# Three of eight row groups summed by TensorE and copied out by ScalarE, the last two groups normalised in one step, and six groups routed first: one gated cross-attention and expert block

## The reference, cut to what matters

```python
# x: (4, 1024, 256); ctx: (4, 77, 256); mask: (1, 1024, 77); 8 experts
x = x + tanh(g_xattn[0]) * xattn(layernorm(x), ctx, ctx, mask, W1, b1, W2, b2)
x = x + tanh(g_ffn[0])   * ffn(layernorm(x), router_w, router_b, w1, w2)

def xattn(q, k, v, mask, ...):          # both projections on q and on k, none on v
    qk = proj(q) @ proj(k).T * 256 ** -0.5 + mask
    return softmax(qk) @ v

def ffn(h, ...):                        # one expert for a token
    route = softmax(h @ router_w + router_b)
    e = argmax(route)
    a, g = split(h @ w1[e])             # 256 -> 2 * 1024
    return (silu(a) * g @ w2[e]) * max(route)
```

## Time and profile before

| what | us |
|---|---|
| median of 3 runs | 448.74 |
| the runs | 448.74, 452.37, 445.57 |
| the profiled execution, as timed | 449.49 |
| its span, first to last instruction | 447.70 |
| PE busy | 401.3 (90% of the span) |
| DVE / ACT / POOL busy | 217.0 / 176.5 / 243.7 |

### The profile page before, as it was taken

The page is one execution under the profiler, slowest core; times in us unless marked ns, Lnnn a source line. Parts: engine busy times, 40 slices in busy tenths (PEclk is TensorE's granted clock), DMA queues, the critical chain, the costliest instruction groups (busy, mean ns, idle before and its releaser), DMA issues.

```text
span 447.7 us, 9834 instructions
## 1 busy us (share of the span) xinstructions
PE 401.3 (90%) x2431; PEld 346.5 (77%) x2432; DVE 217.0 (48%) x527; ACT 176.5 (39%) x338; POOL 243.7 (54%) x324
## 2 busy tenths in 40 slices
PE   5998984149989999999999999999999999999990
PEld 4787872027878888888888888888888888888880
DVE  4689899933454443444433444433444434444340
ACT  1167650024443454545532344445433543233230
POOL 2356997221865577887772258728852676232221
PEclk9999897559999999999999999999999999999996
DMA  7950233863333044333442003433331011000010
GB/s 204 360 199 2 95 107 131 85 175 108 118 118 117 23 166 163 135 117 116 134 155 83 27 17 117 134 112 124 117 117 35 4 35 35 24 24 27 24 33 12
DMA packets 29850, 44.01 MB, mean 98 GB/s; under 512 B 8377, under 2 KB 25581, under 8 KB 27791
## 3 DMA queue, kind: packets, MB, share of 16 engines
q1 hardware_dynamic: 24095, 34.45, 24.6%
q0 software_dynamic: 3456, 9.11, 6.3%
q10 hardware_dynamic: 2288, 0.33, 0.5%
HBM read 35.44 MB, written 8.83 MB: 99 GB/s over the span
## 4 chain that ended last, share of the span: by engine, by line
PE 80%; DVE 7%; POOL 6%; DMA 2%; issue 2%; ACT 1%; DVEq 0%; SPq 0%; POOLq 0%; ACTq 0%
PE py L1117 22%; PE pa L1099 21%; PE pg L1099 21%; PE ph L1109 7%; POOL w_lo L415 2%; PE px L1084 2%; DVE x_all L742 1%; PE ps_s L1024 1%; POOL rstd L399 1%; DMA ctx_in<-in_ctx 1%; DVE bn L750 1%; DMA x_sorted<-residual_rows,idx_gather 1%; PE ps_p L968 1%; PE ps_xt L940 1%; DVE x_norm L878 1%
## 5 line engine op out<-in xcount | busy, mean ns | idle before, releaser
L895 DVE TENSOR_TENSOR ht_lo<-ph,ht_hi 128x512 fp32r<-128x512 f32 x70 | 48.4, 691 | 135.4 <-ACT ht_hi L624 135.4
L493 POOL TENSOR_TENSOR w_lo<-staging,w_hi x84 | 107.1, 1304 | 7.3 <-ACT w_hi L645 4.0
L624 ACT CAST ht_hi<-ph 128x512 fp32r<-128x512 f32 x70 | 41.1, 586 | 118.6 <-PE ph L1109 83.4
L1117 PE MATMUL py<-w_hi,ht_hi 128*128 x280 | 81.3, 291 | 0.8 <-DVE out_tile L903 0.8
L1117 PE MATMUL py<-w_lo,ht_hi 128*128 x280 | 78.4, 280 | 0.0
L1117 PE MATMUL py<-w_hi,ht_lo 128*128 x280 | 78.3, 280 | 0.0
L482 POOL DMA_INDIRECT out<-out_tile,idx_now x34 | 34.6, 1019 | 72.6 <-DVE out_tile L903 72.0
L1099 PE MATMUL pa<-w_hi,xt_hi 128*128 (+1 forms) x140 | 58.7, 420 | 0.8 <-ACT xt_hi L606 0.8
L443 POOL DMA_INDIRECT x_sorted<-residual_rows,idx_now x34 | 35.6, 1048 | 39.5 <-DVE x_norm L878 21.4
L1099 PE MATMUL pg<-w_lo,xt_hi 128*128 (+1 forms) x140 | 55.9, 400 | 0.0
L1099 PE MATMUL pg<-w_hi,xt_hi 128*128 (+1 forms) x140 | 55.9, 399 | 0.0
(11 more groups left out here) (168 smaller groups left out, 583.2 us busy)
## 6 DMA issues: line engine op xcount, KB each, us to landing
staging<-in_L_ffn_w SPq DMA_DIRECT2D x24, 1024.0 KB
residual_rows<-x_all SPq DMA_DIRECT2D x8, 516.0 KB, 4.0
x_all<-in_x SPq DMA_DIRECT2D x8, 512.0 KB, 10.1
x_sorted<-residual_rows,idx_now POOLq DMA_INDIRECT x34
out<-out_tile,idx_now POOLq DMA_INDIRECT x34, 2.5
w_in<-in_L_xattn_W SPq DMA_DIRECT2D x2, 256.0 KB, 4.7
ctx_in<-in_ctx SPq DMA_DIRECT2D x1, 308.0 KB
mask_in<-in_fside_1xSxS ACTq DMA_DIRECT2D x1, 308.0 KB, 11.7
```

What stands on the lines that cost most here:

```text
L493: lo = nc.gpsimd.tensor_tensor(out=w_lo[:, bass.ds(dst + q * QW, QW)], in0=staging[:, bass.ds(src + q * QW, QW)], in1=w_hi[:, bass.ds(dst ...
L624: nc.scalar.copy(ht_hi[:, j], ph[j][:]).then_inc(hhi_ready[j], 1)
L895: nc.vector.tensor_tensor(out=ht_lo[:, j], in0=ph[j][:], in1=ht_hi[:, j].bitcast(FP32), op=ALU.subtract).then_inc(hlo_ready[j], 1)
L1117: last = mm(py[:, 0:D], ht[:, j, c * P:(c + 1) * P], w[:, bass.ds(slot + (DC * PW + (j * HC + c) * D), D)], start=j == 0 and n == 0, stop= ...
```

## The change

In the last three groups (g of 5, 6, 7; `SUMMED` = 5) DVE no longer adds. The probabilities are scaled by the inverse sum before they are transposed (by ACT for groups 5 and 6, four instructions each, by DVE in one instruction for group 7). PE adds the old row itself: into the same `ps_o` bank it first multiplies `x_all` by the identity, then adds the attention product. ACT copies the bank to `x_all`. To have the inverse early, `invert_sums` of groups 4 to 7 moves up two iterations, and in the last iteration `attend(6)` goes ahead of `transpose_probs(7)`. `norm2` takes groups 6 and 7 together, and the iota tables are made behind it. DVE routes groups 0 to 5 first and then 6 and 7. The multiplication by the token's number for the first round moves from POOL to DVE, behind `slot_hot`.

```diff
@@ -51,9 +51,10 @@
     COLS = MAXT + 2
     HALF = 512
     HC = HALF // P
-    PARTS = ((0, NG - 1), (NG - 1, NG))
+    PARTS = ((0, NG - 2), (NG - 2, NG))
     ROUNDS = ((0, 3), (3, 6), (6, NG))
     FIRST = 4
+    SUMMED = NG - 3
     RES = 4
     RW = D + 1
     assert N <= 4096 and B % 2 == 0
@@ -111,7 +112,7 @@
         mv1 = sb1("mv1", [P, NG, B, 2])
         rstd1 = sb1("rstd1", [P, NG, B])
         bn2 = sb1("bn2", [P, 2, B, 6])
-        mv2 = sb1("mv2", [P, 2, B, 2])
+        mv2 = sb1("mv2", [P, 3, B, 2])
         rstd2 = sb1("rstd2", [P, NG, B])
         var_eps1 = sb1("var_eps1", [P, NG, B])
         var_eps2 = sb1("var_eps2", [P, 2, B])
@@ -131,7 +132,7 @@
         expert_m8 = sb1("expert_m8", [P, E])
         token_v = sb1("token_v", [P, NT], FP16)
         part_iota = sb1("part_iota", [P, 1])
-        logit_tmp = sb1("logit_tmp", [P, B, E])
+        logit_tmp = sb1("logit_tmp", [P, 2 * B, E])
 
         prep = ExitStack()
         sb0 = buffers(prep, nc.sbuf_tensor)
@@ -261,6 +262,8 @@
         attn_psum = sem("attn_psum")
         x_logits_ready = sem("x_logits_ready")
         x1_ready = sem("x1_ready")
+        probs_scaled = sem("probs_scaled")
+        rows_copied = sem("rows_copied")
         bn2_ready = sem("bn2_ready")
         mv2_ready = sem("mv2_ready")
         route_step = sem("route_step")
@@ -273,7 +276,6 @@
         gate_ready = sem("gate_ready")
         iotas_ready = sem("iotas_ready")
         col_ready = sem("col_ready")
-        token_ready = sem("token_ready")
         hot_ready = sem("hot_ready")
         logits_ready = sem("logits_ready")
         gate_stored = sem("gate_stored")
@@ -392,21 +394,26 @@
                                         in1=mask_in[:, g:g + 1, :].to_broadcast([P, B, KEYS]),
                                         op=ALU.add).then_inc(mask_c_ready, 1)
 
-            def norm2(g):
-                r = g % 2
-                pool.wait_ge(mv2_ready, g + 1)
-                link(nc.gpsimd.tensor_scalar(var_eps2[:, r], mv2[:, r, :, 1], EPS, None, ALU.add))
-                link(nc.gpsimd.tensor_tensor(out=rstd2[:, g], in0=var_eps2[:, r], in1=minus_half[:, 0:B], op=ALU.pow))
-                link(nc.gpsimd.tensor_tensor(out=logit_tmp[:], in0=x_all[:, g, :, KEPT:XROW],
-                                             in1=rstd2[:, g].unsqueeze(2).to_broadcast([P, B, E]), op=ALU.mult))
-                if g == 0:
+            def norm2(first_group, end_group):
+                n = end_group - first_group
+                at = slice(first_group, end_group)
+                means, variances = (mv2[:, first_group % 2::2][:, 0:n, :, k] for k in range(2))
+                var_eps = var_eps2[:, 0:n]
+                logit = logit_tmp[:, 0:n * B].rearrange("p (g b) e -> p g b e", b=B)
+                pool.wait_ge(mv2_ready, end_group)
+                link(nc.gpsimd.tensor_scalar(var_eps, variances, EPS, None, ALU.add))
+                link(nc.gpsimd.tensor_tensor(out=rstd2[:, at], in0=var_eps,
+                                             in1=minus_half[:, 0:n * B].rearrange("p (g b) -> p g b", b=B), op=ALU.pow))
+                link(nc.gpsimd.tensor_tensor(out=logit, in0=x_all[:, at, :, KEPT:XROW],
+                                             in1=rstd2[:, at].unsqueeze(3).to_broadcast([P, n, B, E]), op=ALU.mult))
+                if first_group == 0:
                     pool.wait_ge(router_b_loaded, 16)
-                nc.gpsimd.tensor_tensor(out=logits[:, g * B:(g + 1) * B], in0=logit_tmp[:],
-                                        in1=router_b_all[:].unsqueeze(1).to_broadcast([P, B, E]),
-                                        op=ALU.add).then_inc(logits_ready, 1)
-                nc.gpsimd.tensor_copy(x_all[:, g, :, 1], rstd2[:, g])
-                nc.gpsimd.tensor_tensor(out=x_all[:, g, :, 0], in0=mv2[:, r, :, 0], in1=rstd2[:, g],
-                                        op=ALU.mult).then_inc(rstd2_ready, 1)
+                nc.gpsimd.tensor_tensor(out=logits[:, first_group * B:end_group * B], in0=logit_tmp[:, 0:n * B],
+                                        in1=router_b_all[:].unsqueeze(1).to_broadcast([P, n * B, E]),
+                                        op=ALU.add).then_inc(logits_ready, n)
+                nc.gpsimd.tensor_copy(x_all[:, at, :, 1], rstd2[:, at])
+                nc.gpsimd.tensor_tensor(out=x_all[:, at, :, 0], in0=means, in1=rstd2[:, at],
+                                        op=ALU.mult).then_inc(rstd2_ready, n)
 
             def low0(c):
 
@@ -422,16 +429,18 @@
             mask1(0)
             mask1(1)
             norm1(EARLY - 1, EARLY)
-            for i in range(NG + 2):
+            for i in range(NG + 1):
                 if 2 <= i + 1 < NG:
                     mask1(i + 1)
                 if i < NG - EARLY:
                     norm1(EARLY + i, EARLY + i + 1)
-                if 0 <= i - 2 < NG:
-                    norm2(i - 2)
+                if 0 <= i - 2 < NG - 2:
+                    norm2(i - 2, i - 1)
+                if i == NG:
+                    norm2(NG - 2, NG)
                 if 0 <= i - 1 < N_CHUNK:
                     low0(i - 1)
-                if i == NG - 1:
+                if i == NG:
                     pool.wait_ge(first_stored, 16 * FIRST)
                     nc.gpsimd.iota(slot_iota[:], [[1, P], [0, B]], base=0, channel_multiplier=0,
                                    allow_small_or_imprecise_dtypes=True)
@@ -446,12 +455,6 @@
             def last_row(t):
 
                 return N - 1 if isinstance(t, int) else pool.snap((t >> 6) + (N - 1))
-
-            end_group = ROUNDS[0][1]
-            pool.wait_ge(col_ready, 1)
-            nc.gpsimd.tensor_tensor(out=col_hot[:, 0:end_group], in0=col_hot[:, 0:end_group],
-                                    in1=token_of[:, 0:end_group].unsqueeze(2).to_broadcast([P, end_group, COLS, B]),
-                                    op=ALU.mult).then_inc(token_ready, 1)
 
             pool.wait_ge(first_stored, 16 * FIRST)
             pool.wait_ge(rows_stored, 16 * (NG - FIRST))
@@ -576,15 +579,34 @@
                                                 accum_out=prob_sum[:, r, b:b + 1])
                 last.then_inc(probs_ready, 1)
 
+            def scale_probs(g):
+                act.wait_ge(inv_ready, g + 1)
+                for b in range(B):
+                    last = nc.scalar.activation(probs[:, g % 2, b], probs[:, g % 2, b], ACT.Copy,
+                                                scale=prob_inv[:, g % 2, b:b + 1])
+                last.then_inc(probs_scaled, 1)
+
+            def copy_rows(g):
+                for b in range(B):
+                    act.wait_ge(attn_psum, B * g + b + 1)
+                    nc.scalar.copy(x_all[:, g, b, X0:XROW], ps_o[(B * g + b) % 3][:, 0:XW]).then_inc(rows_copied, 1)
+
             for i in range(NG + 1):
+                if SUMMED <= i - 1 < NG - 1:
+                    scale_probs(i - 1)
                 if i + 1 < NG:
                     copy_xt(i + 1)
+                if i == NG:
+                    copy_rows(i - 2)
                 if 0 <= i - 1 < NG:
                     copy_pt(i - 1)
+                if SUMMED <= i - 2 and i < NG:
+                    copy_rows(i - 2)
                 if i < NG:
                     softmax(i)
                 if i < N_CHUNK:
                     high0(i)
+            copy_rows(NG - 1)
 
 
             for part, (first_group, end_group) in enumerate(PARTS):
@@ -745,24 +767,38 @@
 
             def stats2(g):
                 r = g % 2
-                dve.wait_ge(x1_ready, B * (g + 1))
-                for b in range(B):
+                into = 2 if g == NG - 1 else r
+                if g < SUMMED:
+                    dve.wait_ge(x1_ready, B * (g + 1))
+                for b in range(B):
+                    if g >= SUMMED:
+                        dve.wait_ge(rows_copied, B * (g - SUMMED) + b + 1)
                     last = nc.vector.bn_stats(bn2[:, r, b], x_all[:, g, b, X0:KEPT])
                 last.then_inc(bn2_ready, 1)
                 dve.wait_ge(bn2_ready, g + 1)
-                if g >= 2:
+                if 2 <= g < NG - 1:
                     dve.wait_ge(rstd2_ready, g - 1)
                 for b in range(B):
-                    last = nc.vector.bn_aggr(mv2[:, r, b], bn2[:, r, b])
+                    last = nc.vector.bn_aggr(mv2[:, into, b], bn2[:, r, b])
                 last.then_inc(mv2_ready, 1)
 
             for i in range(NG + 2):
                 if i < NG:
                     mask_and_max(i)
-                if 0 <= i - 2 < NG:
+                if 0 <= i - 2 < SUMMED - 1:
                     invert_sums(i - 2)
+                if 0 <= i - 2 < SUMMED:
                     add_attention(i - 2)
+                if 0 <= i - 2:
                     stats2(i - 2)
+                if i == SUMMED:
+                    invert_sums(SUMMED - 1)
+                if SUMMED <= i < NG:
+                    invert_sums(i)
+                if i == NG - 1:
```

(46 more changed lines are left out.)

## The result

| | before | changed |
|---|---|---|
| median of 20 runs each | 449.36 us | 453.36 us |
| lowest to highest | 445.57 to 452.37 | 449.85 to 456.88 |
| the profiled execution, its span | 447.7 | 451.7 |

The changed kernel is 4.0 us slower: ratio 1.009, 95% interval 1.0065 to 1.0115 (+2.9 to +5.2 us). The forecast was +2.9 us.

A forecast was written before the change was run, and what follows sets the result against it. It took the start of TensorE's expert stage, set by VectorE's chain for groups 5 to 7, as what could move; 2.0 + 0.9 + 0.4 + 0.1 + 0.15 - 0.67 = +2.9 us gave 451.6 us, range 447.4 to 455.5.

The forecast's parts named there:

- The adds leave VectorE, TensorE gets the path: Attention, groups 5 to 7: 5.5 us of adds leave VectorE; TensorE paces at 0.89 us a tile, 4.0 a group against 3.7.
- the rival of a cheap identity: Attention stage: identity product at 0.12 us, so VectorE sets the pace again; 448.1 us; chance 0.17 with other not-slower cases.
- The wait loop: Attention stage: transposes of groups 5 and 6 wait for ScalarE's scaling, TensorE stands 1.9 us; variance of group 7 +2.0 us.
- The clock, +0.9: Attention stage: TensorE's clock may fall to half after its wait, costing 0 to +1.7 us; +0.9 taken.
- norm2 for two groups: After attention: norm2 of groups 6 and 7 is on the path, pow over eight numbers; 0 to +0.85 us, +0.4 taken.
- the logit instructions: After norm2: two instructions grow from 32 to 64 numbers, +0.1 us.
- Part 1: Routing of the last groups: 64 numbers instead of 32 in five instructions, +0.15 us.
- The iotas: Behind norm2: 1.8 us of iotas, wanted 6 us later; 0 taken, up to +0.6 us if VectorE blocks on them.
- The multiplication, -0.67: Routing, round 1: removing POOL's multiplication gives 1.09 us back at col_hot, VectorE's own adds 0.42; -0.67 us.
- The stores of groups 6 and 7 leave together ... hidden with over 5 us: Before the gathers: two 516 KB stores leave at about 82 us, gathers wait for lists at about 95; no cost.
- signs of being wrong: Profile after: VectorE still without gaps there, identity products under 0.2 us, or a chain through softmax or a store.
- Behind it every microsecond counts once: Expert stage, nearly all of TensorE's busy time: the change moves only its start, and each microsecond there counts once.

The follow-up runs named there:

- e1: Changed kernel with norm2 for single groups, seven groups routed first and the multiplication on GpSimd, all as before; only the summation kept: ratio 1.0075, +3.4 us over the kernel before.
- e4: Changed kernel with attend(4) and attend(5) moved ahead of the transposes and ScalarE's copies reordered to match: ratio 1.0014, +0.6 us against the kernel before.
- e7: Changed kernel with norm2 for single groups and seven groups routed first; summation by TensorE and multiplication on VectorE kept: ratio 1.0050, +2.2 us over the kernel before.
- e6: Changed kernel with SyncE issuing the four gate stores ahead of the row stores of groups 6 and 7: ratio 1.0137, +6.2 us over the kernel before.
- e3: Changed kernel with its four gate stores issued from ScalarE's queue instead of SyncE's: ratio 1.0215, +9.7 us over the kernel before.
- e5: Kernel before with only the multiplication by token number of round 1 moved from GpSimd to VectorE: ratio 0.9990, -0.5 us, not told from zero.
- e2: Changed kernel with VectorE adding in all eight groups as before, the rest of the change kept: ratio 1.0014, +0.6 us over the kernel before, not told from zero.
- e9: Changed kernel without the identity products, read only for its attention stage: 17.1 us from mask_c(7) to the variance of group 7.
- e10: Kernel of e5 with the second weight load issued only after the first gather landed: ratio 0.9986, -0.6 us against the kernel before, median 447.97 us.
- e8: Kernel of e4 with norm2 for single groups and seven groups routed first: median 451.27 us against 450.71 of the kernel before; ratio 0.9943, taken as inconclusive.
- e11: Kernel of e8 with the second weight load issued only after the first gather landed: ratio 0.9959, -1.8 us, median 447.37 against 449.03 of the kernel before.

## Why the prediction was right or wrong

- **The adds leave VectorE, TensorE gets the path: right.** 0.45 us a product, 0.89 a tile, as priced; the rival of a cheap identity fell.
- **The wait loop: right.** I had transposes of group 5 and 6 waiting for ScalarE's scaling, TensorE standing 1.9 us and the stage at +2.0. (The invert of group 4 moves up one iteration, as I walked it, and only those of 5 to 7 two.) Without a fall of the clock the trace of e1 has 1.89 us and +2.5. e4 shows that the order alone causes the wait, and that most of the loss goes with it: -3.4 us.
- **The clock, +0.9: too small for the trace.** In the changed kernel it fell, and the stage took 4.1 more instead of 2.5; e7's fell too, e1's and e6's didn't. That is between 0 and +1.7, as bounded; e3's +3.1 lies outside.
- **norm2 for two groups: right in size.** pow took 1.73 instead of 1.19 us, +0.54 for the +0.4 taken; the logit instructions added nothing that counts, so the stretch is +0.6 for +0.5. Part 1 came at 1.26 instead of 1.08 us, +0.18 for +0.15. The iotas hid.
- **The multiplication, -0.67: right in the trace.** From the first col_hot to the last 4.67 us instead of 5.36. In e5's median it can't be told from zero.
- **The step that failed: "The stores of groups 6 and 7 leave together ... hidden with over 5 us".** The row stores did hide: the second landed at 89.1, 4.7 us ahead of the lists. I followed them and not the gate stores behind them. Those had 0.9 us of cover in the kernel before, not 5. Behind two row stores the last one landed 2.1 us after the lists, and the gather waited 3.2 instead of 1.0 us. That is one of my own signs of being wrong, a chain through a store. The +2.2 of that one trace was partly given back because the gather took 0.8 less. In medians the pair costs 1.8 us, give or take 1.9 (changed kernel against e7), or 1.1, give or take 1.5 (e2 against e5), where I had 0.65.
- **"Behind it every microsecond counts once": not so.** The tail behind the first x_norm runs from 348.7 (e1) to 351.8 us (e2) over the traces (without e9), and it is 0.9 longer in the changed kernel, at nothing in my sum. In the pair before and changed, and in e5 and e10, it is TensorE's clock coming back later.

So +2.9 stands against +4.0 (2.9 to 5.2). The direction and the wait loop held, and the experiments show them: the summation costs +3.4 and reordering takes 3.4 off. The missing microsecond can't be given to one term. In the profiled pair the like-for-like loss is 6.5, 3.6 over my sum: 1.2 in the stage, 1.4 at the gather, 0.9 in the tail and 0.1 in norm2. The medians are too coarse to say how much of each they hold, so that the number came out within 1.1 us is in part luck.

## What to carry to other kernels

Moving work to an engine with slack pays only if that engine's own time for it is below what the path engine spent: here 0.89 us a tile replaced 0.45 of adds in a group that took 3.7 us, and 4.0 is more. Yet this was the small part, 0.6 us of the stage. Before an operation goes in front of a transpose, look at what stands behind the transpose in the queue; putting the ready work first was worth 3.4 us here. And of a store that is made to leave later, follow every transfer behind it to the wait that needs it last. Two traces of one kernel can start 2.5 us apart: compare from landmark to landmark.

## What the runs showed of the hardware that I had not expected

- Four stores of 1024 scattered writes of 4 bytes each took 7.6 to 9.7 us from the first issue to the last landing where none or one row store stood in front (before, e1, e5, e6, e7, e8, e10, e11), and 10.2 to 12.0 us behind two (changed, e2, e4, e9). Issued from ScalarE's queue with a 1 MB load in front they took 16.7 (e3). A 516 KB row store behind them took 12.2 us, where one took 7.4 behind another row store (e6, e3).
- The first gather of 128 rows took 5.7 to 5.9 us where a 1 MB load was issued 0.6 to 0.9 us behind it, and 3.1 to 4.0 where the load came 1.1 us behind or later. That is up to 2.8 us between two traces by chance of order. In the medians no gain from it could be shown (e10 against e5).
- Behind the same wait of 1.89 us TensorE's clock fell in four traces (changed, e3, e7, e9) and not in two (e1, e6). With the identity products it came back 3.4 us after its fall, in e3 6.8; with the 77-row products alone (e9) it stayed at 0.50 for over 10 us, though TensorE showed as busy for the whole of 64 to 72 us in all of them. Why is open.
- The clock comes back at different distances behind the first work of the expert stage, 4.8 to 7.5 us behind the first x_norm, and with it 1 us of the tail comes and goes.
